# A routed tile's second block as two blocks of 32 rows on two column quarters, beside the first block on a column half

## The reference, cut to what matters

```
# L0: 32 experts, 4 per token, inner width 192, one shared expert
g = silu(einsum('th,eih->tei', xf, gate_w)); u = einsum('th,eih->tei', xf, up_w)
routed = einsum('tei,ehi,te->th', g * u, down_w, combine)
# L1: 8 experts, 2 per token, inner width 176, a shared expert of width 352
h = silu(xf @ w1[e].T) * (xf @ w2[e].T);  eo = h @ w3[e].T;  y = sum over the chosen e of comb * eo
```

## Time and profile before

| | us |
|---|---|
| runs | 398.46 and 400.9, median 399.68 |
| the profiled execution | 398.21, of which the span from first to last instruction is 396.4 |
| PE busy | 330.4 of the span |
| DVE, ACT, POOL busy | 271.0, 194.0, 180.7 |
| L0's tiles | from about 92 to 217 |
| L1's tiles | from about 313 to 367 |

### The profile page before, as it was taken

One profiled execution on the slowest core, in us unless ns is written; L12 is line 12 of the kernel. 1 busy time (PEld: TensorE's weight loads), 2 busy tenths in 40 slices (PEclk: granted clock), 3 DMA queues, 4 the chain that ended last, 5 costly groups with the idle time before them and its releaser, 6 DMA issues.

```text
span 396.4 us, 8440 instructions
## 1 busy us (share of the span) xinstructions
PE 330.4 (83%) x2392; PEld 193.7 (49%) x2392; DVE 271.0 (68%) x842; ACT 194.0 (49%) x452; POOL 180.7 (46%) x321
## 2 busy tenths in 40 slices
PE   0007877777999999999999959999877689998997
PEld 0006763443455555555555756666553345554455
DVE  2998869724676766666667596999877246677374
ACT  1349544335455555555551047999921255552110
POOL 2000002266677777777744145666600547774200
PEclk9999957989999999999999979999995899999999
DMA  8999999616933333333563679910011213331441
GB/s 240 345 253 340 251 336 247 166 55 180 310 106 98 105 99 108 107 102 97 131 219 134 239 262 276 223 44 2 2 50 58 79 53 95 109 94 63 155 154 53
DMA packets 35038, 59.88 MB, mean 151 GB/s; under 512 B 4178, under 2 KB 23346, under 8 KB 34994
## 3 DMA queue, kind: packets, MB, share of 16 engines
q1 hardware_dynamic: 26850, 40.41, 34.9%
q0 software_dynamic: 6528, 17.83, 14.8%
q10 hardware_dynamic: 1616, 1.11, 1.0%
HBM read 47.28 MB, written 12.06 MB: 150 GB/s over the span
## 4 chain that ended last, share of the span: by engine, by line
PE 63%; DVE 15%; issue 6%; DMA 5%; POOL 5%; ACT 5%; DVEq 1%; ACTq 0%; SPq 0%; POOLq 0%
PE bank L1388 21%; PE bank L1417 7%; PE bank L1249 6%; PE bank L1431 4%; PE bank L1400 4%; PE bank L1370 4%; PE bank L1482 3%; PE bank L1470 3%; DMA xg<-m_xn,tab 2%; POOL xg L515 2%; PE bank L1262 2%; DMA x_sb<-x 2%; DVE x_sb L1068 1%; PE bank L1162 1%; PE bank L1288 1%
## 5 line engine op out<-in xcount | busy, mean ns | idle before, releaser
L1388 PE MATMUL bank<-arena,xT 128*64 x272 | 94.4, 491 | 2.2 <-ACT xT L647 2.2
L1390 PE MATMUL bank<-xn,xT 128*64 128x384 f32 (+1 forms) x272 | 94.5, 492 | 0.0
L515 POOL DMA_INDIRECT xg<-m_xn,tab x68 | 66.2, 973 | 52.4 <-DVE tab L909 24.8
L504 POOL DMA_INDIRECT m_ys<-ysb,dest x68 | 67.8, 997 | 34.7 <-issue 18.0
L636 ACT ACTIVATE xn<-arena 128x768 f32 (+1 forms) x68 | 56.2, 827 | 18.3 <-issue 17.8
L1388 PEld LDWEIGHTS bank<-arena,xT 128*64 128x64 f32 x272 | 35.0, 139 | 43.9 <-issue 43.9
L992 DVE COPY ysb<-bank 128x256 f32<-128x256 f32 x68 | 26.1, 420 | 39.3 <-PE bank L1433 39.1
L654 ACT ACTIVATE sg<-bank 128x192 f32<-128x192 f32 (+1 forms) x71 | 22.7, 319 | 37.6 <-PE bank L1390 31.7
L647 ACT ACTIVATE xT<-bank 128x512 f32<-128x512 f32 (+1 forms) x36 | 21.3, 592 | 36.0 <-PE bank L1370 36.0
L959 DVE COPY xn<-arena 64x256 f32 (+1 forms) x136 | 36.6, 307 | 1.0
L1417 PE MATMUL bank<-arena,hT 128*64 x136 | 35.0, 380 | 1.7 <-DVE dn L955 1.7
(11 more groups left out here) (197 smaller groups left out, 664.8 us busy)
## 6 DMA issues: line engine op xcount, KB each, us to landing
arena<-w_gu SPq DMA_DIRECT2D x3, 3456.0 KB, 21.9
arena<-m_ys SPq DMA_DIRECT2D x8, 512.0 KB, 5.8
arena<-w_dn SPq DMA_DIRECT2D x6, 576.0 KB, 14.1
arena<-w_gu SPq DMA_DIRECT2D x2, 1408.0 KB
arena<-w_dn SPq DMA_DIRECT2D x3, 864.0 KB, 22.4
m_xn<-xn SPq DMA_DIRECT2D x2, 1024.0 KB, 9.8
arena<-m_ys SPq DMA_DIRECT2D x8, 256.0 KB, 3.3
arena<-w_dn SPq DMA_DIRECT2D x7, 192.0 KB, 9.5
```

Source lines behind the costliest of these rows:

```text
L504: nc.gpsimd.indirect_dma_start(out=ys_d[L.name], out_offset=bass.IndirectOffsetOnAxis(ap=dest[:, s:s + 1], axis=0), in_=ysb[:, s % BUFS, : ...
L515: nc.gpsimd.indirect_dma_start(out=xg[:, b, :], out_offset=None, in_=xn_d[L.name], in_offset=bass.IndirectOffsetOnAxis(ap=d["tab"][:, s:s ...
L1388: T.matmul(out[0:BLOCK, 0:2 * J2], xT[:, s % 4, c, 0:BLOCK], arena[:, bass.ds(off + c * 2 * J2, 2 * J2)], start=(c == 0), stop=(c == C - 1 ...
L1390: ins = T.matmul(out[BLOCK:P, 0:2 * J2], xT[:, s % 4, c, BLOCK:P], gu2[:, s % 2, cols], start=(c == 0), stop=(c == C - 1), tile_position=( ...
```

## The change

In the three products of block 1 (gate and up, down, tail) the 64 stationary rows are cut into two sets of 32, and each set gets a matmul of its own with the same moving operand: one on columns 64 to 95, one on columns 96 to 127, where one matmul on columns 64 to 127 stood. Block 0 keeps its matmul on columns 0 to 63. The semaphore that the block's last product raised is now raised by the second of the two. Nothing else moves.

```diff
-                        ins = T.matmul(out[BLOCK:P, 0:2 * J2], xT[:, s % 4, c, BLOCK:P], gu2[:, s % 2, cols],
-                                       start=(c == 0), stop=(c == C - 1), tile_position=(0, BLOCK))
+                        for r in (BLOCK, BLOCK + 32):
+                            ins = T.matmul(out[r:r + 32, 0:2 * J2], xT[:, s % 4, c, r:r + 32], gu2[:, s % 2, cols],
+                                           start=(c == 0), stop=(c == C - 1), tile_position=(0, r))
                     ins.then_inc(m["g_done"], 1)
...
-                        T.matmul(y[BLOCK:P, 0:H], hT_pair[:, at + BLOCK:at + P], dn2[:, t, :], start=True, stop=False,
-                                 tile_position=(0, BLOCK))
+                        for q in (BLOCK, BLOCK + 32):
+                            T.matmul(y[q:q + 32, 0:H], hT_pair[:, at + q:at + q + 32], dn2[:, t, :], start=True, stop=False,
+                                     tile_position=(0, q))
...
-                        T.matmul(y[BLOCK:P, 0:H], hT_pair[r, P + BLOCK:2 * P], tails[r, 1, :], start=False, stop=True,
-                                 tile_position=(t * BLOCK, BLOCK)).then_inc(m["d_done"], 1)
+                        for q in (BLOCK, BLOCK + 32):
+                            ins = T.matmul(y[q:q + 32, 0:H], hT_pair[r, P + q:P + q + 32], tails[r, 1, :], start=False,
+                                           stop=True, tile_position=(t * BLOCK, q))
+                        ins.then_inc(m["d_done"], 1)
```

## The result

The changed kernel takes 618.43 us (616.26 and 620.61) where the kernel before takes 399.68: a ratio of 1.546, 95% interval 1.525 to 1.566. The forecast was 617. The profiled execution is the slower of the two, 620.61 with a span of 618.9.

A forecast was written before the change was run, and what follows sets the result against it. PE's own pace in both tile stages was taken as the bound; 220.6 us over 24 L0 and 10 L1 pairs, less 3 for waits, on 398.2 gave 615.8, with 1.5 for the median 617; range 540 to 690.

The forecast's parts named there:

- the half that was named as a sign: Tile stages: if the forecast is right, ACT and DVE are idle for half of the stage.
- the bounds: Block 0 beside block 1's quarters: below, array shared, 0.01 us per group; above, one after the other with gaps (taken).
- Passes: Pair of L0: 8 more in gate and up (2.58 us), 4 in first down products (0.87), 6 in tails (1.30).
- Changes of shape: Pair of L0: 0.14 us into 64 columns, 0.12 into 32; 2.22 us in all, 1.80 more than before.
- The three parts: Gate and up, first down products and tails: expected 3.62, 1.25 and 1.68 us more for a pair of L0.
- The start of the quarters: In the timeline, the quarters' first start lies some 0.75 us behind block 0's first, not 0.01.
- The 3 us taken off for waits: Start of the stages: longer passes would cover PE's 2.7 us idle behind a late gather; 3 us taken off.
- Side by side: Rival in the tile pairs: separate columns run together without a gap, under 1 us more, 400 us; chance 0.16.
- Cheaper by collected shapes: Rival in the tile pairs: PE collects products of one shape and pays few gaps, about 545 us; chance 0.14.
- Dearer by alternating passes: Rival in the tile pairs: blocks alternate pass by pass, changing shape within each pair of passes, 688 us; chance 0.10.
- The clock held: Tile stages: the granted clock should hold, as at 1.00 in the attention; something else, such as a lower clock, had 0.02.

The follow-up runs named there:

- quarters everywhere: Changed kernel with block 0 cut into quarters of 32 too, so all three products have four pieces of one shape; 398.38 us, 0.990 of the kernel before.
- one quarter: Changed kernel without block 1's second quarter (rows 96 to 127) from each mixture's third tile on; 622.96 us, ratio 1.550 to the kernel before.
- in order by shape: Changed kernel with products of one shape put behind each other: in gate and up within a tile, 598.30 us; in the tails within a pair, 579.33 us.

## Why the prediction was right

- What bounds the kernel: PE in both tile stages, before and after. What the change cost in the pairs, 220.9 us, came out at the end nearly whole: the medians are 218.75 us apart, the profiled spans 222.5. ACT and DVE are idle for more than the half that was named as a sign, 74% and 69% of the window.
- The choice between the bounds was the step on which all hung: one after the other and not side by side. It held. That a change of shape stops PE also between separate columns was argued from gaps between overlapping pieces; the runs with quarters everywhere and with one quarter show it: four products of one shape start within 0.02, two of unequal shape 0.79 apart (166.44 to 167.23). The Trainium skill, "TensorEngine Tiling (Array Packing)", Key Properties, says that a change of tiling mode drains the engine; the trace agrees, with some 0.09 us of idle array at each change. That tiles run independently, as the same section says, holds in these runs only among pieces of one shape.
- Passes: 8 more a pair of 0.323 us in gate and up (0.297 in L1), 4 and 6 more of 0.217 in the down products and the tails. Changes of shape: 0.14 into 64 columns, 0.12 into 32. The sum for a pair of L0 is 11.65, measured 11.66. A pair of L1 took 5.10 less 8 times the 0.026 by which its passes are shorter, 4.89; with 6.34 more that is 11.23, measured 11.24. The three parts came out at 3.66, 1.24 and 1.66 (3.62, 1.25 and 1.68).
- The start of the quarters was put at some 0.75 us behind block 0's; it is 0.79. The terms already say so (0.37 + 0.323 + 0.09), the sentence rounded them wrongly, and nothing hung on it.
- The 3 us taken off for waits were too much. Of the 2.7 us in which PE was idle between 90 and 101 only half is the late gather's. The timeline before, then the changed kernel's:

```profile
92.58 0.55 PE L1400 MATMUL bank<-ident,hh 128*128 128x128 f32 x3 [1.36 <-DVE hh L971]
...
99.81 0.44 PE L1370 MATMUL bank<-ident,xg 128*128 128x128 f32 x2 [1.36 <-DMA xg<-m_xn,tab]
```

```profile
98.89 0.55 PE L1401 MATMUL bank<-ident,hh 128*128 128x128 f32 x3 [1.36 <-DVE hh L971]
99.27 0.60 PE L1370 MATMUL bank<-ident,xg 128*128 128x128 f32 x4
```

The longer passes covered the wait for the gather; the one for DVE's product (`hh`) is as long as before.
- Against the profiled execution the forecast was 615.8; that one took 620.61 and the other run 616.26. By the pairs alone the span should have grown by 24 x 6.56 + 10 x 6.35 = 220.9 less what waits cover, and it grew by 222.5. That 617 lies within 1.5 us of the median is partly luck: the two runs are 4.4 us apart, the term for waits was too large, and a lower clock at the start (below) was in no term. The agreement of the pairs to 0.01 us is not luck.
- The rivals. Side by side: fell in the pair of the timeline above (its price is given twice, as 0.5 us and as under 1; 34 x 0.02 to 0.03 is 0.7 to 1.0, and nothing hung on it). Cheaper by collected shapes: fell with the two runs in order by shape, which gained just what the order saved. Dearer by alternating passes: the groups are x2 and x4, so block 0's two passes stay together.
- The clock held in the pairs, with 1.00 in the window of L0's, but not in the first pair of the profiled execution:

```profile
86.00:94.00 8.00, 7.23 (x19) 2.03 (x20) 0.42 (x1) 2.14 (x4) 3.65 (x5) 0.57 0.19 56
```

```profile
88.42 1.54 PE L1388 MATMUL bank<-arena,xT 128*64 x2 [0.77 <-ACT xT L647]
...
93.76 0.86 PE L1388 MATMUL bank<-arena,xT 128*64 x2
```

A mean of 0.57 means that most of this stretch ran at the lower level, 1.2 GHz. Four groups take 5.34 us there (88.42 to 93.76) and 3.11 later (158.11 to 161.22): 2.2 us more. The shapes are not shown to be the reason: the run with one quarter has the same shapes and 1.00 from 86 to 95, and in both PE had been busy for some 1.7 of the 3 us from 83 to 86. How much of the 4.4 us between the two runs this is, isn't shown, as the other was not profiled.

## What to carry to other kernels

Before two small products are put side by side on the array, look at whether their pieces have the same rows and columns. In these runs (float32, granted clock 1.00) pieces of one shape shared the array, and one piece of another shape among them put them one after the other, at the price of the passes that no longer overlapped and 0.12 to 0.14 us for each change. If shapes must mix, put products of one shape behind each other in the code, since PE kept to the order of shapes there. Count the changes of shape in a loop that PE bounds: the kernel before has three in a pair, by these prices 0.42 of 5.10 us (an estimate), and a version with fewer was not tried.

## What the runs showed of the hardware that was not expected

The parting was seen for rows as well as for columns: a tail of 32 by 64 in rows 0 to 31 and one of 64 by 64 in rows 64 to 127 ran one after the other, 0.31 us from the second pass of the one (143.93) to the first of the other (144.24), where two tails of 64 by 64 start within 0.02. And within one shape the passes of two products alternate: block 1's first starts before block 0's second when both are halves (140.99 and 141.35). When block 1 comes in quarters, its first starts behind both of block 0's (the x2 at 159.67, the x4 at 160.46).
